# Graph transformer block on one core: node products every second closing gather, Q copies on ScalarE, penalty work on every second step

## The chip, the cores and the metric

The kernel is written by hand for one core of a Trainium2 chip. It uses five engines, each with its own queue of instructions executed in order: TensorE (PE in the profile, its weight loads PEld), VectorE (DVE), ScalarE (ACT), GpSimd (POOL) and SyncE (SP). The last two mostly issue DMAs here. Engines wait for each other on semaphores. The metric is the device time of one execution in microseconds (us).

## The reference

6250 nodes with 256 features, 200000 edges sorted by destination, 8 edge types. Two graph layers follow each other, both with a residual sum and a layer norm around them:

```python
xt = einsum('ni,rio->rno', x, weight)            # layer 0: 8 products for each node
out = segment_sum(xt[edge_type, src_col], row)   # summed over the edges of a node
x = _layernorm(x + relu(out + bias))

Q, K, V = x @ Wq, x @ Wk, x @ Wv                 # layer 1: attention over the edges, 8 heads
score = einsum('ehd,ehd->eh', K[src], Q[dst]) / sqrt(HD) + edge_bias
attn = softmax of score over the edges of each dst
x = _layernorm(x + block(attn-weighted sum of V[src], layer norms, FFN 256-1024-256))
```

## The kernel before, in words

The nodes are cut into W = 49 windows of 128. The program has one long first phase, then the edge phase of layer 1, then the dense part per node.

**Layer 0, gathers.** The edges are sorted by window into T = 1568 lists of 128; W = 49 more lists, the closing ones, hold what is left over of each window, so there are ITEMS = 1617. GpSimd issues an indirect DMA for each (L743, 128 rows of 256 floats) into a ring of 16 tiles in groups of four. TensorE multiplies each tile by a one-hot matrix (`total(i)`, L922) and VectorE adds the result to the window's row in `acc_w` (`add(i)`, L1125). `total` of a closing item waits until the add of the item two before it is done; there are two PSUM banks for them.

**The middle stage.** As soon as closing item j is added, window j is complete. For every window the stage does: on VectorE the relu and the residual sum (`relu_add`, L1329), batch statistics (`count` L1334, `moment` L1338), one over the deviation (`root` L1342) and the normalisation (`normal` L1346); on ScalarE the square root (`deviation`, L1581); on TensorE two transposes (`turn`, L1510), the K and V product (L1537, 512 columns) and the Q product (L1543, 256 columns), both in float32, which the profile shows as two passes for each product; on ScalarE the copy of the transposed tile (`turned`, L1570) and of K and V (L1595); on VectorE the copy of Q into `acc_w` (L1471). SyncE stores the normalised window (L1276, 128 KB) and K and V (L1278, 256 KB), and reloads a ring of x tiles (L1254).

The order of all this is written out by hand. VectorE's part is `norm(m)`: step m starts window m and finishes parts of the windows m-1 to m-7, `normal(m - 4)` and the Q copy of window m-7 among them. TensorE's part is `products(w)`, which begins with `turn(w + 1)`. Both are interleaved with the closing items by two rules that hang on `PACE`:

```python
LAG, PACE = 3, 3
def vector_step(i): return (j - LAG) // PACE if ... (j - LAG) % PACE == 0 else None
def tensor_step(i): return j // PACE - 7 if j is not None and j % PACE == 0 and j >= 7 * PACE else None
```

So `norm(m)` follows the add of closing item 3m (at item j = 3m + 3), and `products(w)` follows the total of closing item j = 3w + 21. The ten products 0 to 9 lie among the closing items, and the other 39 follow in a loop of their own; of the `norm` steps 16 lie among them and 40 behind.

ScalarE's loop over w has the order `deviation(w + 3)`, `turned(w + 1)`, the K and V copy of w, then from window 22 on three copies of turned edge records (`keep_records`, L1576). The K and V copy waits until the store of window w-2 has landed.

**Extra work in `norm` steps.** The edge phase needs tables that VectorE builds in between: constants (`select_consts`, step 16), the window of each item (`walk_row` L1390, steps 21 to 24, `walk_table` L1395 and L1397, step 25), the ends of the records (`pens_ends` L1401, step 26, which waits for 13 indirect DMAs of GpSimd, L1300), penalties (`pens_flag` L1409 and L1411, `pens_out` L1415 and L1417, steps 27 to 32 one after the other), `carries_out` (step 38), and five passes over the local offsets and weights (L1443, L1492, L1446, L1449, steps 44 to 50). On TensorE `spread` (L1515) follows the products of windows 13 to 16, and `turn_records` (L1527) those of windows 22 to 34.

When all five engines are through, a meeting (`meet`, L354) opens the edge phase. Its first gather is at L1664.

## Time and profile before

| | us |
|---|---|
| median of 3 runs | 6389.73 |
| fastest and slowest of them | 6384.63, 6389.86 |
| span of the profiled execution, first to last instruction | 5325.8 |
| TensorE busy / VectorE busy | 4332.7 (81%) / 4739.1 (89%) |
| ScalarE busy / GpSimd busy | 3258.1 (61%) / 3215.5 (60%) |
| granted TensorE clock, mean over the span | 0.965 |

The times are of runs without the profiler. The page gives no time of the profiled execution but its span. The runs' median lies 1063.9 us above the span, a factor of 1.1998.

### The profile page before, as it was taken

How to read it: one execution, taken by the hardware profiler on the slowest of the kernel's cores; microseconds unless marked ns; L12 is line 12 of the kernel's file. 1: busy time of each engine (PE TensorE's matmuls, PEld its weight loads, DVE VectorE, ACT ScalarE, POOL GpSimd, SP SyncE). 2: the span in 40 equal slices, each digit the busy share in tenths (PEclk: the TensorE clock that was granted, in tenths of full speed). 3: DMA queues.
4: the chain of work that ended last, by engine and by line, in shares of the span. 5: the costliest groups of instructions: out<-in, count | busy, mean ns of one | idle time of the engine just before them, and what ended most of it. 6: DMA issues, size and time to landing. Idle time of an engine off the chain costs nothing.

```text
span 5325.8 us, 88503 instructions
## 1 busy us (share of the span) xinstructions
PE 4332.7 (81%) x19115; PEld 2887.9 (54%) x19115; DVE 4739.1 (89%) x15510; ACT 3258.1 (61%) x8885; POOL 3215.5 (60%) x3370
## 2 busy tenths in 40 slices
PE   8997777777777777666978888888888888888997
PEld 3444444344444444443656666666666666666665
DVE  6888999999999999665679999999999999998666
ACT  3887777777777777300356666666666666663221
POOL 2003777777777777777167777777777777770000
PEclk9999999999999999877999999999999999999999
DMA  6333333333333333436567777777777777772000
GB/s 200 125 120 102 106 106 105 105 105 106 106 105 103 103 103 104 131 105 112 184 202 215 215 214 212 212 210 211 212 209 212 211 210 211 212 212 87 9 16 25
DMA packets 346045, 779.09 MB, mean 146 GB/s; under 512 B 75122, under 2 KB 176519, under 8 KB 345525
## 3 DMA queue, kind: packets, MB, share of 16 engines
q0 software_dynamic: 214608, 659.52, 43.4%
q1 hardware_dynamic: 127285, 111.00, 6.7%
q8 instruction: 174, 2.85, 0.2%
q10 hardware_dynamic: 3632, 2.88, 0.2%
q14 instruction: 346, 2.83, 0.2%
HBM read 691.52 MB, written 81.59 MB: 145 GB/s over the span
## 4 chain that ended last, share of the span: by engine, by line
PE 37%; DVE 29%; issue 16%; POOL 8%; ACT 4%; DMA 3%; DVEq 3%; SPq 0%; ACTq 0%; POOLq 0%
PE pb L1700 11%; POOL big L743 8%; DVE node_a L1848 5%; PE pb L922 4%; PE pb L1684 4%; PE pb L418 4%; DVE walk_s L1059 3%; ACT walk_s L752 3%; PE pb L2103 3%; PE pb L832 2%; DVE big L1804 2%; DMA big<-xt_table,big 2%; DVE big L1013 2%; DVE node_a L1125 2%; PE pb L2092 2%
## 5 line engine op out<-in xcount | busy, mean ns | idle before, releaser
L1664 POOL DMA_INDIRECT big<-kv_table,walk_s x1664 | 1585.2, 953 | 579.9 <-issue 477.8
L743 POOL DMA_INDIRECT big<-xt_table,big x1617 | 1554.6, 961 | 542.5 <-issue 457.0
L752 ACT ACTIVATE walk_s<-walk_s,big 128x128 bf16<-128x128 bf16 x4704 | 1498.8, 390 | 441.0 <-DVE walk_s L1059 416.4
L922 PE MATMUL pb<-big,walk_s 128*128 128x256 f32 x3234 | 1037.1, 416 | 225.0 <-DMA big<-xt_table,big 203.6
L1700 PE MATMUL pb<-big,early 128*128 128x264 f32 x3328 | 841.8, 397 | 98.9 <-issue 83.9
L1125 DVE TENSOR_TENSOR node_a<-node_a,pb 128x256 f32 (+1 forms) x1617 | 661.4, 410 | 209.0 <-PE pb L922 198.4
L1684 PE MATMUL pb<-node_a,hot_t 128*128 x3328 | 820.1, 390 | 29.9 <-issue 23.0
L832 PE MATMUL pb<-walk_s 128*128 128x384 bf16 x1568 | 534.1, 341 | 362.3 <-ACT walk_s L752 329.5
L922 PEld LDWEIGHTS pb<-big,walk_s 128*128 128x128 f32 x3234 | 616.1, 206 | 371.4 <-DMA big<-xt_table,big 277.4
L1700 PEld LDWEIGHTS pb<-big,early 128*128 128x128 f32 x3328 | 603.8, 192 | 220.5 <-issue 118.8
L1684 PEld LDWEIGHTS pb<-node_a,hot_t 128*128 128x128 f32 x3328 | 603.9, 191 | 113.4 <-issue 48.3
L832 PEld LDWEIGHTS pb<-walk_s 128*128 128x128 bf16 x1568 | 153.9, 98 | 824.1 <-ACT walk_s L752 773.0
L1757 ACT ACTIVATE early<-off_e,one_p 128x512 f32<-128x512 bf16 x416 | 300.3, 722 | 487.9 <-PE pb L1700 487.4
L1804 DVE TENSOR_TENSOR big<-big,pb 128x1024 f32<-128x1024 f32 x416 | 504.2, 1212 | 29.1 <-DMA big<-kv_table,walk_s 23.5
L1752 ACT ACTIVATE off_e<-iota_q,walk_s 128x128 bf16<-128x128 f32 x1664 | 525.8, 388 | 0.2
L834 PE MATMUL pb<-walk_s 128*97 128x384 bf16 x1568 | 523.3, 334 | 0.0
L1810 DVE TENSOR_REDUCE big<-big 128x32 f32<-128x1024 f32 x416 | 504.2, 1212 | 0.1
L1834 DVE TENSOR_TENSOR big<-big,pb 128x1024 f32<-128x1024 f32 x409 | 493.4, 1206 | 4.5 <-PE pb L1700 4.5
L1155 DVE TENSOR_SCALAR walk_s<-early,big 128x128 f32<-128x128 int16 x1570 | 472.6, 301 | 8.9 <-ACT node_a L791 7.5
L1059 DVE TENSOR_SCALAR walk_s<-early,big 128x225 bf16<-128x225 int16 x1568 | 473.0, 302 | 0.0
L1058 DVE TENSOR_SCALAR walk_s<-early,big 128x128 bf16<-128x128 int16 x1568 | 427.8, 273 | 39.2 <-PE pb L834 37.2
L1848 DVE SCALAR_TENSOR_TENSOR node_a<-node_a,walk_s,pb 128x264 f32 x832 | 397.6, 478 | 3.6 <-PE pb L1700 2.4
(294 smaller groups left out, 5573.2 us busy)
## 6 DMA issues: line engine op xcount, KB each, us to landing
xt_table<-big SPq DMA_DIRECT2D x98, 512.0 KB, 2.9
big<-kv_table,walk_s POOLq DMA_INDIRECT x1664, 3.7
big<-xt_table,big POOLq DMA_INDIRECT x1617
pens<-pen_table SPq DMA_DIRECT2D x832, 12.1 KB
kv_table<-big SPq DMA_DIRECT2D x49, 256.0 KB, 2.1
x_store<-big SPq DMA_DIRECT2D x49, 128.0 KB, 2.5
big<-in_x POOLq DMA_DIRECT2D x48, 128.0 KB, 3.3
big<-x_store SPq DMA_DIRECT2D x6, 1024.0 KB, 11.9
```

The source lines that it names most:

```text
L743: e.indirect_dma_start(sum_rows[:, q % SUM_ROWS, k, :], None, xt_table, bass.IndirectOffsetOnAxis(ap=idx_all[:, i:i + 1], axis=0))\
L752: ins = e.activation(hot_v[:, t % SORT_HOTS, v, :], hot_q[:, t % SORT_HOTS, :], ACT.Copy, scale=byte[:, t:t + 1])
L832: e.matmul(pb[:, 0, 0:3 * P], hot_c[:, t % SORT_HOTS, 0:P], vals, start=(u == 0), stop=last, skip_group_check=True)
L922: e.matmul(pb[:, bank, 0:D], one_hot, sum_rows[:, q % SUM_ROWS, k, :], start=True, stop=True)\
L1059: e.tensor_scalar(hot_c[:, k, 0:COLS], iota_s[:, 0:COLS], c_c[:, t:t + 1], None, ALU.is_equal)\
L1125: e.tensor_tensor(to, to, pb[:, bank, 0:D], ALU.add).then_inc(added.sem, 1)
L1664: e.indirect_dma_start(rows[:, q % ROW_RING, k, 0:2 * D], None, kv_table, bass.IndirectOffsetOnAxis(ap=src_i[:, i:i + 1], axis=0))\
L1684: ins = e.matmul(pb[:, q % 2 * 2 + k // 2, k % 2 * D:(k % 2 + 1) * D], hot_t[:, q % 2, k * P:(k + 1) * P], acc_q[:, bass.ds(at[k // 2], D) ...
L1700: ins = e.matmul(pb[:, 5 + j, 0:AW], hot_e[:, q % 2, i * P:(i + 1) * P], rows[:, q % ROW_RING, i, D:ROW], start=(k == 0), stop=(k == 1))
L1752: ins = e.activation(off_e[:, k * P:(k + 1) * P], iota_q[:, 0:P], ACT.Abs, bias=dl_f[:, i:i + 1], scale=-1.0)
L1804: e.tensor_tensor(keys, keys, pb[:, q % 2 * 2:q % 2 * 2 + 2, :].rearrange("p b (k n) -> p b k n", k=2), ALU.mult).then_inc(x_mul.sem, 1)
L1848: e.scalar_tensor_tensor(to, to, same_w[:, i:i + 1], pb[:, 5 + j, 0:AW], ALU.mult, ALU.add)\
```

## The change

`PACE` goes from 3 to 2. The Q copy leaves VectorE's `norm` for ScalarE's loop, directly behind the K and V copy. `SPREAD_AT` and `REC_AT` put the spreads and the turned records six windows later (19 and 28). VectorE's table work moves to later steps: `walk_row` 25 to 28, `walk_table` 30, `pens_ends` 31, the six penalty passes 32, 34, 36, 38, 40 and 42, `carries_out` 46. The last passes come behind the last normalisation, in steps 53 to 58.

```diff
-        LAG, PACE = 3, 3
+        LAG, PACE = 3, 2
...
-        NORM_LAG, Q_LAG = 4, 7
-        STEPS_MID = W + Q_LAG
-        REC_AT = 22
+        NORM_LAG = 4
+        SPREAD_AT, REC_AT = 19, 28
+        STEPS_MID = W + NORM_LAG + 6
...
-                w = m - Q_LAG
-                if 0 <= w < W:
-                    e.wait_ge(s_qkv, 2 * w + 2)
-                    e.tensor_copy(acc_w[:, w + 1, 0:D], pb[:, 4 + w % 2, 0:D]).then_inc(s_qc, 1)
...
-                if 21 <= m < 25:
-                    walk_row(m - 21)
-                if m == 25:
+                if 25 <= m < 29:
+                    walk_row(m - 25)
+                if m == 30:
                     walk_table()
-                if m == 26:
+                if m == 31:
                     pens_ends()
-                if 27 <= m < 33:
-                    k, odd = divmod(m - 27, 2)
+                if 32 <= m < 44 and m % 2 == 0:
+                    k, odd = divmod((m - 32) // 2, 2)
...
-                if m == 38:
+                if m == 46:
                     carries_out()
-                if m == 44:
+                late = m - W - NORM_LAG
+                if late == 0:
                     locals_of()
-                if m == 46:
+                if late == 1:
...
-                b = w - 13
+                b = w - SPREAD_AT
...
                 e.activation(kv_out[:, w % 2, :], pb[:, 2 + w % 2, :], ACT.Copy).then_inc(s_kvc, 1)
+                e.wait_ge(s_qkv, 2 * w + 2)
+                e.activation(acc_w[:, w + 1, 0:D], pb[:, 4 + w % 2, 0:D], ACT.Copy).then_inc(s_qc, 1)
```

What this moves, in the order of each engine's instructions. In the changed kernel the lines of the middle stage carry slightly other numbers (L1329 is L1330 there, L1543 is L1541, L1595 is L1593).

VectorE among the closing items, one step, before (L1329 to L1338 are the norm step, L1471 the Q copy, L1125 the adds of closing items):

```order
L1329 SCALAR_TENSOR_TENSOR big<-node_a,big 128x256
L1342 RECIPROCAL rstd<-spread_s 128x1
L1334 BN_STATS stats<-big 128x6
L1346 TENSOR_SCALAR big<-big,mv,rstd 128x256
L1338 BN_AGGR mv<-stats 128x2
L1471 COPY node_a<-pb 128x256
L1125 TENSOR_TENSOR node_a<-node_a,pb 128x256 x3
```

and now:

```order
L1330 SCALAR_TENSOR_TENSOR big<-node_a,big 128x256
L1343 RECIPROCAL rstd<-spread_s 128x1
L1335 BN_STATS stats<-big 128x6
L1347 TENSOR_SCALAR big<-big,mv,rstd 128x256
L1339 BN_AGGR mv<-stats 128x2
L1125 TENSOR_TENSOR node_a<-node_a,pb 128x256 x2
```

The copy has left the step, and two adds lie between norm steps instead of three.

ScalarE in the same place, two windows, before (L1595 is the K and V copy, L1581 the square root, L1570 the copy of the transposed tile):

```order
L1595 ACTIVATE big<-pb 128x512
L1581 ACTIVATE spread_s<-mv,eps_c 128x1
L1570 ACTIVATE big<-pb 128x256
L1595 ACTIVATE big<-pb 128x512
L1581 ACTIVATE spread_s<-mv,eps_c 128x1
L1570 ACTIVATE big<-pb 128x256
```

and now:

```order
L1593 ACTIVATE big<-pb 128x512
L1595 ACTIVATE node_a<-pb 128x256
L1579 ACTIVATE spread_s<-mv,eps_c 128x1
L1568 ACTIVATE big<-pb 128x256
L1593 ACTIVATE big<-pb 128x512
L1595 ACTIVATE node_a<-pb 128x256
L1579 ACTIVATE spread_s<-mv,eps_c 128x1
L1568 ACTIVATE big<-pb 128x256
```

The Q copy (L1595 there) stands between the K and V copy and the square root that the next norm step waits for.

VectorE at the first two penalty passes, before (L1409 and L1415 are the passes):

```order
L1409 TENSOR_TENSOR big<-big 128x13x127
L1329 SCALAR_TENSOR_TENSOR big<-node_a,big 128x256
L1342 RECIPROCAL rstd<-spread_s 128x1
L1334 BN_STATS stats<-big 128x6
L1346 TENSOR_SCALAR big<-big,mv,rstd 128x256
L1338 BN_AGGR mv<-stats 128x2
L1471 COPY node_a<-pb 128x256
L1415 TENSOR_SCALAR big<-big 128x13x127
```

and now:

```order
L1410 TENSOR_TENSOR big<-big 128x13x127
L1330 SCALAR_TENSOR_TENSOR big<-node_a,big 128x256
L1343 RECIPROCAL rstd<-spread_s 128x1
L1335 BN_STATS stats<-big 128x6
L1347 TENSOR_SCALAR big<-big,mv,rstd 128x256
L1339 BN_AGGR mv<-stats 128x2
L1330 SCALAR_TENSOR_TENSOR big<-node_a,big 128x256
L1343 RECIPROCAL rstd<-spread_s 128x1
L1335 BN_STATS stats<-big 128x6
L1347 TENSOR_SCALAR big<-big,mv,rstd 128x256
L1339 BN_AGGR mv<-stats 128x2
L1416 TENSOR_SCALAR big<-big 128x13x127
```

Two norm steps lie between two passes where one lay.

## Rows read from the trace of the kernel before

**Rows 1.** Windows of the middle stage: length, busy PE, PEld, DVE, ACT, POOL, PEclk, DMA, GB/s

```profile
2510.00:2556.00 46.00, 39.19 (x146) 24.78 (x145) 24.25 (x83) 10.46 (x27) 18.27 (x20) 1.00 0.52 159
2557.00:2575.00 18.00, 18.00 (x76) 11.73 (x75) 9.66 (x39) 5.81 (x15) 12.45 (x13) 1.00 0.84 275
...
2500.00:2680.00 180.00, 166.10 (x631) 104.05 (x629) 117.77 (x369) 63.86 (x185) 43.16 (x46) 1.00 0.57 177
```

**Rows 2.** Timeline of PE at closing items 12 to 14 and 21: start, duration

```profile
2501.41 1.91 PE L922 MATMUL pb<-big,walk_s 128*128 128x256 f32 x6 [1.15 <-DMA big<-xt_table,big]
...
2509.60 0.70 PE L922 MATMUL pb<-big,walk_s 128*128 128x256 f32 x2 [0.95 <-DVE node_a L1125]
...
2510.14 0.38 PE L1510 MATMUL pb<-ident,big 128*128 128x128 f32 x2
```

**Rows 3.** Timeline of PE, one whole step among the closing items

```profile
2551.04 0.38 PE L1510 MATMUL pb<-ident,big 128*128 128x128 f32 x2
2551.26 1.88 PE L1537 MATMUL pb<-big 128*128 128x512 f32 x4
2552.98 1.03 PE L1543 MATMUL pb<-big 128*128 128x256 f32 x4
2553.84 1.03 PE L922 MATMUL pb<-big,walk_s 128*128 128x256 f32 x4
2555.62 0.67 PE L922 MATMUL pb<-big,walk_s 128*128 128x256 f32 x2 [0.75 <-issue]
2556.13 0.38 PE L1510 MATMUL pb<-ident,big 128*128 128x128 f32 x2
```

**Rows 4.** Timeline of ACT and DVE in the same step

```profile
2553.18 0.60 ACT L1595 ACTIVATE big<-pb 128x512 f32<-128x512 f32 x1 [1.34 <-PE pb L1537]
2553.67 0.28 ACT L1581 ACTIVATE spread_s<-mv,eps_c 128x1 f32<-128x1 f32 x1
...
2553.99 0.16 DVE L1342 RECIPROCAL rstd<-spread_s 128x1 f32<-128x1 f32 x1 [1.99 <-ACT spread_s L1581]
...
2554.80 0.39 DVE L1471 COPY node_a<-pb 128x256 f32<-128x256 f32 x1
2555.11 0.74 DVE L1125 TENSOR_TENSOR node_a<-node_a,pb 128x256 f32<-128x256 f32 x2
```

**Rows 5.** Waits from 2557 to 2680: total us, times, longest

```profile
ACT big L1595 <- DMA kv_table<-big: 7.4, 3, 3.5
...
PEld pb L1510 <- DVE big L1346: 3.0, 4, 1.5
...
PEld pb L1515 <- DVE big L1390: 0.7, 1, 0.7
```

**Rows 6.** DVE groups of the same stretch: busy us, mean ns, idle before

```profile
L1411 DVE TENSOR_TENSOR big<-big 128x1664 f32<-128x1664 f32 x2 | 6.4, 3180 | 0.0
...
L1449 DVE TENSOR_TENSOR walk_s<-walk_s,big 128x1664 f32<-128x1664 f32 x2 | 3.8, 1880 | 0.0
...
L1446 DVE TENSOR_SCALAR big<-walk_s 128x1664 f32<-128x1664 f32 x2 | 2.0, 1017 | 0.0
```

**Rows 7.** Timeline of DVE, first and last instruction around the constants of step 16

```profile
2560.31 0.39 DVE L1473 MEMSET node_a<- 128x400 f32 x1
...
2562.60 0.43 DVE L1329 SCALAR_TENSOR_TENSOR big<-node_a,big 128x256 f32<-128x256 f32 x1
```

**Rows 8.** Timeline of ACT, copies of turned records

```profile
2601.79 0.61 ACT L1576 ACTIVATE walk_s<-pb 128x128 f32<-128x128 f32 x3
2602.26 0.32 ACT L1581 ACTIVATE spread_s<-mv,eps_c 128x1 f32<-128x1 f32 x1
```

**Rows 9.** L1300, the gathers of records: duration, first and last start; landing

```profile
L1300 POOL DMA_INDIRECT big<-edge_table,t_int x13: 944/946/1064, 2557.5 to 2572.7; - x13
...
DMA to landing us min/median/max: 3.3/5.7/7.0
```

**Rows 10.** Timeline, the last Q product and the first gather of the edge phase

```profile
2678.18 1.03 PE L1543 MATMUL pb<-big 128*128 128x256 f32 x4
...
2681.36 1.03 POOL L1664 DMA_INDIRECT big<-kv_table,walk_s  x1 [46.30 <-SPq L354]
```

More of the change, by code:

```diff
@@ L1234, in build @@
         assert x_marks[FIRST_LOADS] == X_RING and all((hi - 1) // X_RING == lo // X_RING for lo, hi in x_loads[:-1])
-        NORM_LAG, Q_LAG = 4, 7
-        STEPS_MID = W + Q_LAG
-        REC_AT = 22
+        NORM_LAG = 4
+        SPREAD_AT, REC_AT = 19, 28
+        STEPS_MID = W + NORM_LAG + 6
+        assert SPREAD_AT > (W - 1) // PACE - 7 and SPREAD_AT + 4 <= REC_AT and REC_AT + WALK_G < W
         def xs_of(w):
@@ L1486, in norm @@
                         pens_flag(k)
-                if m == 38:
+                if m == 46:
                     carries_out()
-                if m == 44:
+                late = m - W - NORM_LAG
+                if late == 0:
                     locals_of()
-                if m == 46:
+                if late == 1:
                     c(e.tensor_copy(dl_b, dl_f))
-                if m == 47:
+                if late == 2:
                     bias_mask(0.0, ALU.is_lt)
-                if m == 48:
+                if late == 3:
                     bias_add()
-                if m == 49:
+                if late == 4:
                     bias_mask(float(P), ALU.is_ge)
-                if m == 50:
+                if late == 5:
                     bias_add()
```

## The prediction

> **What bounds the kernel now.** I read the page first: no engine is full over the whole span, so the stage decides. The windows came next. All lines that the change touches work between 2500 and 2680 us, where PE is busy 166.1 of 180 us at full granted clock [rows 1]; VectorE, with 117.8 us, is not the bound. So the question is where PE's other 14 us are, and PE's timeline answers it. Among the closing items one step (turn, K and V, Q, three totals) takes 5.09 us from turn to turn [rows 3]; ten such places lie there. Its work is 2.80 us (2551.04 to 2553.84) for a window's products and 3 x 0.43 for the totals (four passes of L922 are 0.86 us apart from the next start, when nothing stalls), together 4.09. From the first turn of the ten (2510.14, [rows 2]) to the one behind them (2556.13) are 9 x 5.11 us. So 1.02 us of a mean step is not work; 0.08 of it is a handover that will stay (below), 0.94 is waiting.
>
> Why it is idle stands in ScalarE's and VectorE's rows [rows 4]. The K and V product ends at 2552.98; its copy starts 0.20 later, the square root 0.49 after that, and VectorE, which had waited 1.99 us for this root, starts at 2553.99. Root to moment takes 0.81, the Q copy 0.31, the first add 0.34, then PE gets its third total (2555.62) and, 0.51 later, the next turn. The whole ring is one step long: products of w release the norm step that stands ahead of the add that the total ahead of products w+1 waits for. Behind the closing items PE runs without a gap (2.80 us a window), except where VectorE is late with penalty passes: 3.0 us before turns and 0.7 before a spread by PEld's rows [rows 5]. From the last Q product (2678.18 + 0.86 = 2679.04) to the edge phase's first gather are 2.3 us [rows 10], which stay as they are: a store landing and the meeting.
>
> **The change, part by part.** The yardstick is the end of the last Q product, 2679.04.
>
> *Earlier start.* Products 0 now follow total 14 instead of total 21. Totals 12 to 14 ran from 2501.41 for 1.91 us, having waited for their rows to land; that wait stays. The turn can start at about 2503.3 instead of 2510.14 [rows 2]: 6.8 us earlier. Seven totals are then still to do, 7 x 0.43 = 3.0 us. Gain 3.8. VectorE can follow: a norm step without the copy is 0.81 + 0.34 (the relu sum has the size of an add), and two adds are 0.68, in all 1.83 us for two items [rows 4].
>
> *The ring opens.* With two items to a step, `norm(w + 6)`, which waits for the root behind products w-1, stands behind the add of item 2w + 12, and the total ahead of products w (item 2w + 14) needs that add alone. It does not wait for this norm step. So the ring is two steps long and holds one pass of about 5.4 us (worked out below), 2.7 for a step, against PE's 2.80 + 2 x 0.43 = 3.66. PE is the bound. The 0.94 us go in all nine steps between products 0 and 9: gain 8.5.
>
> *More handovers.* From the last total to the turn PE takes 0.51 us instead of 0.43 [rows 3]. There are 18 such places instead of 10: loss 8 x 0.08 = 0.6.
>
> *The Q copy on ScalarE.* 49 copies. ScalarE's copy of 512 columns takes 0.49 us to the next start, its copies of 128 take 0.47 / 3 = 0.16 each [rows 4, 8]; 256 columns lie between, 0.27. VectorE gives up 0.31 each, 15 us in all, but none of it at PE's bound outside the ring. The Trainium skill's page "Perfetto Trace Analysis", section Engine Utilization, gives ScalarE 153.6 and VectorE 245.76 G elements a second, a rule against this move: by it 32768 elements take 0.08 us longer on ScalarE, and each of the three late turns below would be later by that, 0.2 us in all. The rows show the fixed parts outweigh this. The square root behind the Q copy comes later: the copy waits for the Q product, 0.86 behind K and V, then 0.20 and 0.27, instead of 0.20 and 0.49. That is 0.64 us later. It is covered by the step gained above: PE needs the norm step a whole step later.
>
> *Penalties every second step.* Behind the closing items PE's step is 2.80, plus 0.33 while records are turned (three transposes at 0.11). VectorE's two steps with one long pass are 2 x 1.15 + 3.2 [rows 6] = 5.5 us, against PE's 5.6 to 6.3. Three such pairs are nearly even, so a few tenths may stay: I take 0.5 us. Of the 3.7 us that go, PE's own gaps between starts show about 3.4. Gain 2.9. The bounds are 0 (the waits stay, 3.4 lost) and 3.7.
>
> *Constants.* Step 16 now falls among the closing items (item 35). It holds VectorE for 2.3 us (2560.31 to 2562.60, [rows 7]), and the next two adds stand behind it. VectorE has 3.66 - 1.83 = 1.8 us to spare in a step, less what it waits for the root; I estimate 0.8 us lost, between 0.5 and 2.3.
>
> *Spreads and records six windows later.* The same instructions, cost 0. The gathers of records start behind the last add, now near 2567: 13 x 1.25 us, then 5.7 to land [rows 9], so at about 2589. `pens_ends` asks for them behind product 24, about 2593. If that margin of 4 us goes, VectorE stands and PE with it.
>
> *The last passes.* They come behind the last normalisation: three of 1.88 and three of 1.02 us [rows 6], 8.7 in all. The last normalisation can go 0.64 us later than before; PE then has the products of windows 47 and 48 ahead, the copy and the store. Before, that normalisation ended some 9.6 us ahead of 2679.04 and 11.9 ahead of the gather; now about 9.0 and 11.3. 8.7 us fit with 2 us to spare. Cost 0; without cover each us beyond it shows in full.
>
> Sum: 3.8 + 8.5 - 0.6 + 2.9 - 0.8 = 13.8, so **14 us** off the span of 5325.8. Direct count as a check: 2503.3 + 49 x 2.80 + 34 x 0.43 + 18 x 0.08 + 3 spreads of 0.89 and one of 0.22 + 13 x 0.33 + 1.3 of waits - 0.22 (the last has no turn) = 2664.9, or 14.1 less than 2679.04.
>
> **From the span to the time.** The median is 1063.9 us above the span, a factor of 1.1998. If what lies around the span is fixed, the time falls by 14; if all stretches by that factor, by 16.8. The trace cannot tell. I take the factor, since the trace shows no stretch outside the program's own work that could be a fifth of it, and keep 14 as the other end. The Trainium skill, "Advanced Engine Details and Errata", section Clock Domains, says that a chip's power profile moves the base clock and names 2.0 beside 2.4 GHz for PE, a factor of 1.2; no row here shows that the timed chip was set so. Forecast: 6389.7 - 16.8 = **6373**.
>
> **The rivals.**
>
> *DMA holds the shorter step.* A step would move 2 x 128 KB of rows, 128 of x1, 256 of K and V and about 128 of x, some 0.79 MB in 3.66 us: 215 GB/s instead of 159. For it: ScalarE waited 7.4 us for K and V stores in the stretch with 275 GB/s at 0.84 of the DMA engines [rows 1, 5]. Against it: by the same row 215 GB/s are 0.66 of them, and PE lost nothing to those waits. If a step took 4.3 us, 17 steps would cost 10.9 us more; gain 3 x 1.2 = 3.7, time 6386. The store would have to land later than about 6 us after its issue.
>
> *Records late.* If the record gathers land in 13 us instead of 5.7, `pens_ends` holds VectorE about 3 us: gain 11 x 1.2 = 13, time 6377. For it: they now share the DMA engines with stores at PE's full rate; against it, they did before too.
>
> *The ring stays closed (slower).* If the norm step ahead of each product still needs the product just before, the Q copy on ScalarE is in the ring. It is then 1.72 (K and V) + 0.86 + 0.20 + 0.27 + 0.29 (to the root) + 0.81 + 0.34 + 0.17 + 0.51 + 0.22, about 5.4 us for two items instead of three. Products 17 would start at 2503.3 + 17 x 5.4 = 2595.1, and 31 more at 2.80 with 7.5 of spreads and records and 1 of waits end near 2693: 14 us later, time 6389.7 + 16.8 = 6406. It decides as soon as a step's slack (3.66 x 2 against 5.4, so 1.9 us) is eaten, say by a late add. The order rows speak against it.
>
> **How the numbers follow.** A measurement of this kernel can tell a difference of about 0.2%, 12.8 us. The forecast gets 0.74: of that 0.70 lie beyond 12.8 us, 0.04 fall short with the factor absent and two terms at their low ends. DMA holds: 0.14, all within 0.2%. Records late: 0.06, 0.02 faster and 0.04 within. Ring closed: 0.06, slower. Faster 0.72, same 0.22, slower 0.06. The range: the best case is all terms at their high ends (start at 2502.9, no waits left, constants 0.5), 15.7 x 1.2 = 18.9 us, and 2.5 of scatter between runs: 6368. At the other end it takes in records late and the milder half of the DMA case, 6382. That leaves out about 0.15.
>
> **What would show it.** Right: from one L1541 row to the next among closing items 3.7 us, no DVE-released idle before L922; the first L1508 turn of window 1 near 2503; the last Q product near 2665; VectorE's last pass ends before the first gather; ScalarE's Q copies start 0.2 behind L1541. Wrong: steps of 4 us or more with ScalarE waiting for stores, or the gaps before L1508 at the penalty passes as long as before; and if all of this holds but the time falls by 14 and not 17, the factor is wrong.

## The result, and the profile after

| | median us | range of the runs |
|---|---|---|
| before, 10 runs | 6389.8 | 6373.9 to 6414.2 |
| after, 10 runs | 6359.6 | 6344.3 to 6383.4 |

The ratio is 0.9952, 95% interval 0.9939 to 0.9965: faster by 30 us (22 to 39). Forecast were 6373 and a range from 6368. The direction is right; the gain is nearly twice the forecast's 17 us, and the time is 8.4 us under the range.

One thing must be known to read the numbers: the runs came in sets of different pace, in which the kernel before takes about 5328, 6390 or 6474 us, run after run. Below, a quick, 6390 or 6474 chip is short for such a set. Whether the pace belongs to the chip isn't shown, since the record gives the 6390 and the 6474 set of the experiments the same chip number. The profile shown ahead of the prediction (span 5325.8) is of the quick kind, the times beside it are of the 6390 kind. In each of the ten runs after, the time is 1.7 to 1.8 us above the span of the same run, so the 1063.9 us between the two were never around the program.

The profile after is of the 6390 kind. Its page begins:

```profile
span 6363.5 us, 88501 instructions
...
PEclk9998888888888888768888888988899888899999
```

Its granted TensorE clock is 0.82 in the gather stage and 0.89 in the edge phase; in the profile before it was 0.93 and 0.99. Its windows (gather stage, touched stage, edge phase, dense last part):

```profile
480.00:2935.00 2455.00, 1636.90 (x6063) 973.02 (x6063) 1834.34 (x8320) 1308.96 (x4067) 1526.58 (x1587) 0.82 0.31 87
2935.00:3115.00 180.00, 167.96 (x629) 107.30 (x629) 98.10 (x309) 77.97 (x231) 46.15 (x49) 0.95 0.55 177
3118.00:5836.00 2718.00, 2043.97 (x9222) 1550.09 (x9223) 2083.26 (x3675) 1428.19 (x3378) 1579.05 (x1664) 0.89 0.57 165
5836.00:6360.00 524.00, 465.21 (x1791) 321.00 (x1790) 365.61 (x1244) 129.90 (x275) 0.76 (x1) 0.97 0.11 32
```

VectorE's busy time in the touched stage fell from 117.8 us [rows 1] to 98.1, ScalarE's rose from 63.9 to 78.0: 49 copies changed sides. PE's timeline, a whole step among the closing items (answers [rows 3]) and the step with the constants:

```profile
2952.47 1.03 PE L1541 MATMUL pb<-big 128*128 128x256 f32 x4
2953.34 1.03 PE L922 MATMUL pb<-big,walk_s 128*128 128x256 f32 x4
...
2956.14 1.03 PE L1541 MATMUL pb<-big 128*128 128x256 f32 x4
...
2985.45 1.03 PE L1541 MATMUL pb<-big 128*128 128x256 f32 x4
2986.94 1.13 PE L922 MATMUL pb<-big,walk_s 128*128 128x256 f32 x4 [0.47 <-DVE node_a L1125]
...
2989.85 1.03 PE L1541 MATMUL pb<-big 128*128 128x256 f32 x4
```

A step is 3.67 us from Q product to Q product, with no idle time; the one with the constants is 4.40. ScalarE and VectorE in the same kind of step (answers [rows 4]):

```profile
2957.20 0.38 ACT L1595 ACTIVATE node_a<-pb 128x256 f32<-128x256 f32 x1 [0.27 <-PE pb L1541]
2957.48 0.28 ACT L1579 ACTIVATE spread_s<-mv,eps_c 128x1 f32<-128x1 f32 x1
...
2957.80 0.16 DVE L1343 RECIPROCAL rstd<-spread_s 128x1 f32<-128x1 f32 x1 [1.80 <-ACT spread_s L1579]
...
2958.60 0.72 DVE L1125 TENSOR_TENSOR node_a<-node_a,pb 128x256 f32<-128x256 f32 x2
```

VectorE still waits 1.8 us for the root, but PE no longer waits for VectorE. The end of the stage (answers [rows 10]): the last pass ends at 3114.61, 2.85 us ahead of the gather, and hides.

```profile
3112.72 1.89 DVE L1450 TENSOR_TENSOR walk_s<-walk_s,big 128x1664 f32<-128x1664 f32 x1
...
3114.30 1.03 PE L1541 MATMUL pb<-big 128*128 128x256 f32 x4
...
3117.46 1.03 POOL L1664 DMA_INDIRECT big<-kv_table,walk_s  x1 [22.84 <-SPq L354]
```

So the mechanism came as forecast. The question is the size: where the other 13 us are from.

### The profile page after: what moved, and what is told of

The parts are those of the page before. It is cut to its first block, busy times and chain, and to the rows that moved or that the text cites. A ratio compares the mean times of both kernels' runs of the same rounds, so it can differ in the third digit from the quotient of the medians.

```text
span 6363.5 us, 88501 instructions
## 1 busy us (share of the span) xinstructions
PE 4755.2 (75%) x19115; PEld 3163.2 (50%) x19115; DVE 4764.5 (75%) x15461; ACT 3290.1 (52%) x8934; POOL 3213.0 (50%) x3370
## 3 DMA queue, kind: packets, MB, share of 16 engines
q8 instruction: 174, 2.85, 0.2%
## 4 chain that ended last, share of the span: by engine, by line
PE 27%; issue 13%; DVE 8%; another core or an unknown queue 5%; DVEq 2%; ACT 2%; DMA 0%; POOL 0%; ACTq 0%; SPq 0%; POOLq 0%
PE pb L1700 11%; PE pb L1684 6%; PE pb L2103 2%; DVE node_a L1848 2%; PE pb L2092 2%; PE pb L922 1%; PE pb L1535 1%; DVEq L336 1%; ACT early L1743 1%; PE pb L2115 1%; PE pb L1675 1%; DVE big L1804 1%; PE pb L1726 1%; PE pb L1541 1%
## 5 line engine op out<-in xcount | busy, mean ns | idle before, releaser
L1664 POOL DMA_INDIRECT big<-kv_table,walk_s x1664 | 1580.4, 950 | 1161.8 <-PE pb L1700 537.6
L743 POOL DMA_INDIRECT big<-xt_table,big x1617 | 1556.5, 963 | 996.7 <-issue 454.1
L922 PE MATMUL pb<-big,walk_s 128*128 128x256 f32 x3234 | 1168.4, 457 | 156.5 <-DVE walk_s L1155 74.3
L1700 PE MATMUL pb<-big,early 128*128 128x264 f32 x3328 | 993.4, 449 | 205.1 <-issue 156.7
L1125 DVE TENSOR_TENSOR node_a<-node_a,pb 128x256 f32 (+1 forms) x1617 | 668.0, 414 | 588.4 <-PE pb L922 245.6
L832 PE MATMUL pb<-walk_s 128*128 128x384 bf16 x1568 | 590.3, 377 | 687.6 <-ACT walk_s L752 478.4
L1684 PE MATMUL pb<-node_a,hot_t 128*128 x3328 | 879.9, 410 | 23.4 <-issue 18.9
L1700 PEld LDWEIGHTS pb<-big,early 128*128 128x128 f32 x3328 | 688.1, 219 | 386.8 <-issue 261.3
L922 PEld LDWEIGHTS pb<-big,walk_s 128*128 128x128 f32 x3234 | 700.3, 232 | 320.5 <-issue 106.6
L1684 PEld LDWEIGHTS pb<-node_a,hot_t 128*128 128x128 f32 x3328 | 651.1, 207 | 124.8 <-issue 43.6
L834 PE MATMUL pb<-walk_s 128*97 128x384 bf16 x1568 | 583.0, 372 | 0.0
```

Of the source, the lines that this page charges most:

```text
L743: e.indirect_dma_start(sum_rows[:, q % SUM_ROWS, k, :], None, xt_table, bass.IndirectOffsetOnAxis(ap=idx_all[:, i:i + 1], axis=0))\
L832: e.matmul(pb[:, 0, 0:3 * P], hot_c[:, t % SORT_HOTS, 0:P], vals, start=(u == 0), stop=last, skip_group_check=True)
L834: ins = e.matmul(pb[0:COLS - P, 1, 0:3 * P], hot_c[:, t % SORT_HOTS, P:COLS], vals, start=(u == 0), stop=last, skip_group_check=True)
L922: e.matmul(pb[:, bank, 0:D], one_hot, sum_rows[:, q % SUM_ROWS, k, :], start=True, stop=True)\
L1125: e.tensor_tensor(to, to, pb[:, bank, 0:D], ALU.add).then_inc(added.sem, 1)
L1664: e.indirect_dma_start(rows[:, q % ROW_RING, k, 0:2 * D], None, kv_table, bass.IndirectOffsetOnAxis(ap=src_i[:, i:i + 1], axis=0))\
```

## The experiments

The comparison below uses one stretch, from the start of the 20th last row gather (L743) to the first edge gather (L1664). All that the change touches lies in it or just before its start. In the profile before it is 172.0 us; the forecast is 14 less.

**Four kernels on a quick chip** (kernel before: 5328.0 us, 33 runs). Run 1 is the kernel before, unchanged.

> The kernel before, unchanged, to get its trace in the condition in which the changed kernel was traced (span 6363.5 us, where the first trace of the kernel before had 5325.8). Theory A (pauses): its span is near 6385, its engines show pauses of 2 to 5 us that no other engine's work explains, and its middle stage, from the first closing total to the first gather of the edge phase, is 25 to 35 us longer than the changed kernel's (about 190 us): the closed ring of one step passes every pause on to TensorE, the open one takes part of it up. Theory B (elsewhere): the middle stages differ by 14 us as forecast and the rest of the 30 us lies in the two long stages around it. Time: no change, 6389 us.

Measured 5327.8 us, ratio 1.0001 (0.9992 to 1.0010), span 5321.7. The kernel repeats within 0.1%. It fell into a quick set, so it couldn't show how the kernel before looks where it takes 6390 us, and neither theory was decided.

Run 2 is the changed kernel with the Q copies back on VectorE, at their old lag:

```
                if 0 <= m - 2 < W:
                    moment(m - 2)
+                w = m - 7
+                if 0 <= w < W:
+                    e.wait_ge(s_qkv, 2 * w + 2)
+                    e.tensor_copy(acc_w[:, w + 1, 0:D], pb[:, 4 + w % 2, 0:D]).then_inc(s_qc, 1)
...
-                e.wait_ge(s_qkv, 2 * w + 2)
-                e.activation(acc_w[:, w + 1, 0:D], pb[:, 4 + w % 2, 0:D], ACT.Copy).then_inc(s_qc, 1)
```

> The changed kernel with the Q copy back in the norm step of VectorE (seven steps behind, as before). Both theories: the closing steps stay at 3.67 us, since VectorE has room for 0.31 us more in a step. The late passes now share VectorE with the last Q copies and cannot end before the last Q product and copy, so VectorE ends some 5 us behind TensorE and the stage's end moves by about 4 us. If the copy's place matters only there: 4 x 1.2 = 5 us slower than the changed kernel, 6365 us. If moving the copy had been worth its 15 us of VectorE time: 6375 us.

Measured 5318.5 us, ratio 0.9984 (0.9975 to 0.9993), stretch 163.8 us. PE's steps among the closing items are 3.66 us as with the copy on ScalarE, so the pace opens the ring by itself. But the late passes now end after PE. Timelines of its end:

```profile
2666.01 1.03 PE L1545 MATMUL pb<-big 128*128 128x256 f32 x4
...
2667.14 0.42 DVE L1472 COPY node_a<-pb 128x256 f32<-128x256 f32 x1 [1.22 <-PE pb L1545]
...
2671.52 1.89 DVE L1450 TENSOR_TENSOR walk_s<-walk_s,big 128x1664 f32<-128x1664 f32 x1
...
2673.74 1.03 POOL L1666 DMA_INDIRECT big<-kv_table,walk_s  x1 [27.61 <-DVEq L354]
```

The last Q copy waits for the last Q product, the passes queue behind it, and the edge phase meets them at 2673.4. From last Q product to gather are 7.7 us instead of 3.2. So the move to ScalarE is worth 4.5 us at this place. The stretch is 6.2 us longer than that of the changed kernel in run 10 (157.6): another 1.6 us are longer waits at the penalty passes, where VectorE has 0.31 us more to do for each window. Without the move over a third of the 16.2 us that the whole change gains on a quick chip is given back.

Run 3 has the new places (spreads, records, penalty steps, late passes) with the old pace and the Q copies on VectorE. Against the changed kernel, with the lines of the Q copy as in run 2:

```
-        LAG, PACE = 3, 2
+        LAG, PACE = 3, 3
...
+                w = m - 7
...
```

> The kernel before with the table work of VectorE, the spreads and the turned records at their new places alone (PACE 3, Q copy on VectorE). The closed ring stays: steps among closing items 5.1 us. The waits at the penalty passes go (2.9 us), but the late passes end some 5 us behind the last Q product and give it back. Theory A: no change within 5 us, 6389 us. A theory in which the spread penalty work is the source of the surplus gain: 6370 us or less.

Measured 5330.3 us, ratio 1.0002 (0.9993 to 1.0011), stretch 180.2. The steps are 5.07 as before, and the same 4.5 us stand at the end. The new places alone gain nothing.

Run 4 is the changed kernel with the old pace:

```
-        LAG, PACE = 3, 2
+        LAG, PACE = 3, 3
```

> The changed kernel with PACE 3 again (Q copy on ScalarE, table work at its new places). The closed ring is back and holds the wait for the Q product: steps of 5.4 us instead of 5.1, nine of them, 3 us; the waits at the penalty passes are gone, 3 us. So as before or up to 3 us slower: 6389 to 6393 us under theory A, where nearly all of the 30 us is the pace. If the pace is worth only what the forecast gave it (11 of 14 us), the time is 6376.

Measured 5329.8 us, ratio 1.0004 (0.9995 to 1.0013), stretch 177.2. In the closed ring the Q copy on ScalarE costs. One step in its timelines:

```profile
2521.53 1.03 PE L1541 MATMUL pb<-big 128*128 128x256 f32 x4
2522.39 1.03 PE L922 MATMUL pb<-big,walk_s 128*128 128x256 f32 x4
2524.52 0.70 PE L922 MATMUL pb<-big,walk_s 128*128 128x256 f32 x2 [1.10 <-DVE node_a L1125]
...
2526.99 1.03 PE L1541 MATMUL pb<-big 128*128 128x256 f32 x4
...
2522.59 0.38 ACT L1595 ACTIVATE node_a<-pb 128x256 f32<-128x256 f32 x1 [0.27 <-PE pb L1541]
2522.88 0.29 ACT L1579 ACTIVATE spread_s<-mv,eps_c 128x1 f32<-128x1 f32 x1
```

The step takes 5.46 us here, 5.40 in the mean, against 5.07: the root is later by 0.64, the copy's 0.31 on VectorE is saved, 0.33 remain. Pace two is what gains; pace three with the rest of the change gains nothing.

**Four kernels on a 6390 chip** (kernel before: 6390.0 us, 27 runs). Run 5 is the changed kernel again:

> The changed kernel once more, unchanged. On a chip that runs the kernel before in about 5328 us (as the first four runs did) the middle stage's terms alone decide. Theory A (the change is worth the 14 us of the middle stage, and the surplus came with the slow-paced execution): 5314 us, ratio 0.9973, last Q product 160 us behind the first (before 166). Theory B (the change is worth 30 us anywhere): 5298 us, ratio 0.9944. If the chip runs the kernel before in about 6390 us again: A and B both 0.995, and the trace must say in which stage the surplus lies.

Measured 6366.0 us, ratio 0.9966 (0.9949 to 0.9983): 24 us, and 11 to 33 by the interval. Stretch 165.1, as in the first profile after (165.2). Its first step among the closing items is a long one, though the ring is open:

```profile
2945.75 1.03 PE L1541 MATMUL pb<-big 128*128 128x256 f32 x4
...
2949.66 1.19 PE L922 MATMUL pb<-big,walk_s 128*128 128x256 f32 x2 [2.15 <-issue]
...
2955.96 1.12 PE L1541 MATMUL pb<-big 128*128 128x256 f32 x4
```

It is 10.21 us instead of 3.66.

Run 6 is the kernel before with nothing changed but the Q copies, which go to ScalarE (the lines of run 2 the other way round, pace three):

> The kernel before with the Q copies on ScalarE alone (three items to a step, penalty passes as before). The ring is closed, so the copy's place in it counts: ScalarE's square root comes 0.64 us later, VectorE's copy of 0.31 is gone, so a step of the ten is 5.07 + 0.33 = 5.40 us, 9 x 0.33 = 3.0 us more; behind the closing items VectorE gains 0.31 a window, which takes about 1 us off the penalty waits. Expected +2 us (0 to +3), 5330 us, ratio 1.0004. The rival, that the Q copy is a burden of VectorE which PE pays for: a step of 4.8 us, 3 us less, 5325.

Measured 6389.4 us, ratio 0.9993 (0.9978 to 1.0008). Behind a first step of 11.35 us the steps are 5.38 to 5.47, as expected (5.40), and the rival's 4.8 is out. Its stretch takes 190.0 us: 24.8 more than the changed kernel's on that chip, where I had 14, or 16 with this kernel's own loss of about 2 us.

Runs 7 and 8 have stalls of VectorE put in, first the kernel before, then the changed one:

```
+                if m in (7, 9, 11, 13):
+                    for _ in range(4):
+                        c(e.memset(acc_w[:, :, D:AW], 0.0))
```

> The kernel before with four artificial stalls of 1.86 us on VectorE (four 0.46 us memsets of the same columns behind norm steps 7, 9, 11 and 13, while products 1 to 7 run). If the ring is closed, each is paid in full: 4 x 1.86 = 7.4 us, 5335.4 us, ratio 1.0014, and four of the ten steps become 6.9 us instead of 5.1. If VectorE has room in a step (it waits 2 us for the root), nothing: 5328 us.

Measured 6397.6 us, ratio 1.0014 (1.0000 to 1.0029): 7.5 us more, at the edge of what these runs can tell.

> The changed kernel with the same four stalls of 1.86 us behind norm steps 7, 9, 11 and 13, again while products 1 to 7 run. If the ring is two steps long and holds 5.4 us of 7.3, a stall is absorbed: at most 0.3 us each, so at most 1.2 us above the changed kernel (5315 us against 5314). If the ring is closed at heart and only shorter, each is paid in full: 7.4 us, 5321 us. The difference between what the stalls cost before and after (7.4 against 1) is what an open ring saves where an engine pauses.

Measured 6362.8 us, 3 us under run 5 and not told apart from it (ratio to before 0.9957, 0.9941 to 0.9974). The answer is in the traces. The memsets stand 0.54 apart, so a stall is 2.17 us and not 1.86. In the kernel before (run 7) the last stalled step is 7.24 us instead of 5.07: paid in full. The other three are longer, 8.88, 8.72 and 9.80 us. PE's timeline of the third and the fourth, and the windows behind their waits:

```profile
3001.74 1.19 PE L922 MATMUL pb<-big,walk_s 128*128 128x256 f32 x2 [3.08 <-issue]
...
3003.16 3.62 PE L1540 MATMUL pb<-big 128*128 128x512 f32 x4
...
3016.45 0.70 PE L922 MATMUL pb<-big,walk_s 128*128 128x256 f32 x2 [2.88 <-DVE node_a L1125]
...
3017.20 1.88 PE L1540 MATMUL pb<-big 128*128 128x512 f32 x4
```

```profile
3001.70:3006.60 4.90, 4.86 (x9) 2.54 (x10) 1.03 (x3) 0.38 (x1) 0.00 (x0) 0.50 0.05 13
3016.40:3020.00 3.60, 3.55 (x13) 2.37 (x14) 1.15 (x4) 1.16 (x3) 0.00 (x0) 1.00 0.00 0
```

PE waited 2.9 to 3.1 us in all four. Behind three of these waits the granted clock was 0.50 to 0.61, the K and V product took 2.68 to 3.62 us instead of 1.88, and VectorE got its root later; behind the fourth it stayed at 1.00. The four stalls, 8.7 us in all, cost PE 14.4 us.

In the changed kernel (run 8) the first stall falls into the long first steps and can't be read. The other three make steps of 4.35 us instead of 3.67: 0.69 each, more than the 0.3 expected, a third of the stall. VectorE's total of two steps, 2 x 1.83 + 2.17, is 5.8 of 7.3 us, but the stalled step alone (4.0) is longer than PE's. PE's waits there are 0.42 us, and the granted clock stays at 1.00.

**Four kernels on a quick chip again** (kernel before: 5329.8 us, 21 runs). Run 9 is the kernel before, run 10 the changed one.

> The kernel before, unchanged, for its stages beside the next run's. If this chip paces the gather stages slowly (6390 us): from the start of the 20th last row gather (L743) to the first edge gather (L1664) 185 to 190 us, where a quick chip takes 172 to 174; ratio 1.000. On a quick chip 5328 us and 172 to 174.

Measured 5327.5 us, ratio 0.9995 (0.9986 to 1.0004), stretch 175.1.

> The changed kernel, unchanged. Theory A (the terms of the middle stage are right, and the surplus of the first result is what a slow-paced chip adds to a slower start and a closed ring, plus scatter between executions of the untouched stages): on a slow-paced chip 20 to 24 us less than the run of before from the 20th last row gather to the first edge gather, and differences of either sign and under 10 us in the two stages on its sides; ratio about 0.9963. On a quick chip 14 us less in that stretch and in the whole, ratio 0.9973. Theory B (something in the gather or edge stages gets faster with the change): the stretch gives 14 us on either chip, and 10 us or more come again from one and the same untouched stage.

Measured 5308.3 us (5 runs), ratio 0.9964 (0.9950 to 0.9977): 19 us, 12 to 27. The stretch of run 9 and then of this one, in the windows' columns:

```profile
2508.70:2683.80 175.10, 161.56 (x618) 101.79 (x617) 111.88 (x349) 63.38 (x183) 36.11 (x39) 1.00 0.56 175
```

```profile
2505.00:2662.60 157.60, 154.38 (x605) 100.29 (x603) 92.99 (x290) 76.56 (x225) 36.68 (x40) 1.00 0.60 192
```

PE stands still for 3.2 of 157.6 us, where it was 13.5 of 175.1. The three quick traces of the kernel before (172.0, 174.2, 175.1) have a mean of 173.8, so the change takes 16.2 off it. Everything outside the stretch (span less stretch) took 5155.3 us in run 9 and 5148.6 in this one. The other seven quick traces lie between 5147.5 and 5155.2, those of the kernel before among them. So no change of the stages around it is seen.

Run 11 is the kernel before with products w behind item 3w + 18 instead of 3w + 21:

```
-            return j // PACE - 7 if j is not None and j % PACE == 0 and j >= 7 * PACE else None
+            return j // PACE - 6 if j is not None and j % PACE == 0 and j >= 6 * PACE else None
...
-                if i == T + 6 * PACE:
+                if i == T + 5 * PACE:
...
-            for w in range((W - 1) // PACE - 6, W):
+            for w in range((W - 1) // PACE - 5, W):
```

> The kernel before with one thing changed: products w follow item 3w + 18 instead of 3w + 21 (still every third item). The total ahead of products w then needs only adds ahead of norm step w + 5, whose root stands behind products w - 2, so the ring is two steps long at this pace too. If the ring was what held the step: steps of 2.80 + 3 x 0.43 + 0.08 = 4.17 us instead of 5.07, ten times, 9 us, and 1.6 us of an earlier start: 11 us, 5317 us on a quick chip, ratio 0.998. If the pace of three was at fault (VectorE's three adds and a norm step), steps of 5.07 stay and 1.6 us are gained: 5326 us, ratio 0.9997.

Measured 5321.5 us, ratio 0.9990 (0.9981 to 0.9999), stretch 165.6: 8.2 us less than 173.8, where 11 were expected. The steps are 4.45 us, neither 5.07 nor 4.17. PE's and VectorE's timelines tell why:

```profile
2533.51 1.81 PE L922 MATMUL pb<-big,walk_s 128*128 128x256 f32 x6
2535.16 0.38 PE L1510 MATMUL pb<-ident,big 128*128 128x128 f32 x2
...
2534.15 0.85 DVE L1125 TENSOR_TENSOR node_a<-node_a,pb 128x256 f32<-128x256 f32 x2 [1.37 <-PE pb L922]
```

Three totals take 1.65 us, 0.55 each, not 0.43. There are two banks, so the third waits for the add of the first, 0.28 us more than forecast for the step. Of the old step of 5.07 the ring cost 0.62 and the third total 0.28. The 0.94 that the prediction gives to the ring, from a mean step of 5.11, had these two parts, and a pace of two removes both.

Run 12 is the changed kernel with the same shift, to item 2w + 12, and the constants moved behind the closing items (steps 23 and 24):

> The changed kernel with products w behind item 2w + 12 instead of 2w + 14, and the constants of step 16 behind the closing items (the memset in step 23, the others in step 24). Two items' worth of earlier start, of which PE waited some 1 to 2 us for rows, and the 0.74 us of the constants: 2 us better than the changed kernel on a quick chip (5312 us, ratio 0.997), 3 us on a slow-paced one. The step of 4.40 us at product 10 becomes 3.66. If the norm step ahead of the turn is late instead, steps of 4 us or more between products, and no gain.

Measured 5313.1 us (5 runs), ratio 0.9965 (0.9951 to 0.9978); stretch 156.2 against 157.6. All seventeen closing steps are 3.66 or 3.67. But the turn behind the last one waits, since its norm step stands behind the last add of the phase and not behind the add of item 46:

```profile
2567.46 0.44 PE L1509 MATMUL pb<-ident,big 128*128 128x128 f32 x2 [1.59 <-DVE big L1347]
```

The 2 us that were expected on top of the changed kernel don't show: run 10 took 5308.3 us in the same set.

**Four kernels on a 6474 chip** (kernel before: 6474.2 us, 27 runs). Run 13 is the kernel before again, run 14 the changed one.

> The kernel before, unchanged. On a quick chip: 5328 us, the stretch from the 20th last row gather to the first edge gather 172 to 175.1 us as in three traces so far. On a slow-paced chip: 6390 us and 185 to 190 us in that stretch.

Measured 6471.0 us, ratio 1.0002 (0.9990 to 1.0015), stretch 186.2.

> The changed kernel, unchanged. If the surplus is scatter of the untouched stages: the stretch takes 157 to 159 us on a quick chip (16 less than before), 165 on a slow-paced one (20 to 24 less), and the stages on its sides differ by under 8 us with a sign that changes between pairs. If the change reaches them: 5 us or more less in the same stage as in the pairs so far (the last dense part was 3 us shorter in the tenth run, the gather stage 6 us shorter on the slow-paced chip).

Measured 6442.2 us, ratio 0.9959 (0.9944 to 0.9974), stretch 167.1. The windows of run 13 and then of this one, gather stage, stretch, edge phase:

```profile
479.00:2992.00 2513.00, 1640.84 (x6079) 978.31 (x6080) 1839.09 (x8336) 1307.95 (x4070) 1532.36 (x1598) 0.82 0.31 86
2992.00:3177.00 185.00, 165.20 (x617) 103.62 (x615) 112.49 (x349) 63.17 (x183) 35.73 (x39) 0.98 0.52 165
3178.00:5940.00 2762.00, 2055.49 (x9225) 1558.29 (x9222) 2082.55 (x3675) 1428.00 (x3378) 1575.13 (x1664) 0.88 0.57 162
```

```profile
479.00:3001.00 2522.00, 1644.27 (x6094) 984.67 (x6095) 1840.93 (x8342) 1310.40 (x4076) 1529.02 (x1598) 0.82 0.31 85
3001.00:3167.00 166.00, 157.79 (x602) 101.73 (x600) 92.92 (x290) 75.98 (x225) 36.25 (x39) 0.98 0.57 182
3167.00:5916.00 2749.00, 2052.14 (x9221) 1555.53 (x9222) 2081.20 (x3675) 1425.23 (x3377) 1575.07 (x1663) 0.88 0.57 163
```

The stretch is 19 us shorter; the stages beside it differ by +9 and -13. Both are more than the 8 expected, but of opposite sign, and neither stage differs the same way in all pairs of traces. Run 16 below is the same kernel as this one, and its gather stage and edge phase differ from this one's by 11 and 16 us: so large is the scatter of stages that nobody touched.

Run 15 is the kernel of run 12 with the late norm step put right and the constants in steps 25 and 26:

```
+            m = (W - 1 - LAG) // PACE + 1
             for i in range(ITEMS - LAG, ITEMS):
                 add(i)
-            for m in range((W - 1 - LAG) // PACE + 1, STEPS_MID):
+                if closing(i) == PACE * m:
+                    step.norm(m)
+                    m += 1
+            for m in range(m, STEPS_MID):
                 step.norm(m)
...
```

> The twelfth kernel (products w behind item 2w + 12) with norm step 23 behind the add of item 46, where the pattern has it, instead of behind the last add, and the constants in steps 25 and 26, where a step of PE is 3.69 us. The turn that waited 1.59 us behind norm step 23 in the twelfth run waits for nothing: the stretch 154.7 us instead of 156.3 on a quick chip (the changed kernel: 157.6), 3 us less than the changed kernel in all, 5310 us, ratio 0.9967. If something else holds that turn, 156.3 stays.

Measured 6450.5 us, ratio 0.9974 (0.9961 to 0.9987). The turn waits no more: the step that was 5.47 us in run 12 is 3.66. The stretch is 164.9, 2.2 and 2.8 us under those of runs 14 and 16, but the time isn't lower. A gain of 3 us is below what these runs can tell, so it doesn't count as a better version. Run 16 is the changed kernel once more.

> The changed kernel once more, so that two traces and two sets of times of it stand beside each other: as the fourteenth, within 0.1% of it in time; the stretch within 2 us of the fourteenth's.

Measured 6448.7 us, ratio 0.9967 (0.9956 to 0.9978), stretch 167.8; within 0.1% of run 14, as expected.

## Why the prediction was right in kind and wrong in size

| chip (kernel before) | stretch before | stretch after | less | all outside it, before / after | time, less |
|---|---|---|---|---|---|
| 5328 | 172.0, 174.2, 175.1 | 157.6 | 16.2 | 5147.5 to 5155.3 / 5148.6 | 19 (12 to 27) |
| 6474 | 186.2 | 167.1, 167.8 | 18.8 | 6280.2 / 6275.8, 6279.9 | 27 (17 to 36), 21 (14 to 29) |
| 6390 | 190.0 (Q copies on ScalarE) | 165.2, 165.1 | 24.8 | 6198.4 / 6198.3, 6196.1 | 31 (22 to 39), 22 (11 to 33) |

The last column is worked out from the ratios. Their mean, weighted by the intervals, is 0.38%: 20 us of 5328, 24 of 6390.

On a quick chip the terms can be checked one by one. They add up to 16.2 us where 13.8 were forecast.

*Earlier start, 3.8.* Right, and a little more. The first K and V product starts 0.9 to 2.7 us behind the 20th last gather before and 5.8 ahead of it after: 7.7 earlier in the mean, forecast 6.8.

*The ring opens, 8.5, and handovers, -0.6.* Right in cause, and a little more in size. PE's step is 3.66, forecast 3.74: there is no handover cost at two totals. What I called a handover of 0.08 is not seen there. This gives most of another 1.2 us. Run 11 shows the other misreading: 0.28 of the old wait was the third total in a row, not the ring. Both go, so the sum is hardly touched.

*Q copy on ScalarE, 0.* Right for the closing steps: run 2 has 3.66 us there with the copy on either engine, because the ring is open. Where it is closed, the copy on ScalarE costs 0.33 a step (runs 4 and 6), 3 us in all. What the prediction doesn't say is that the late passes hide only because the copy has left VectorE (run 2: 4.5 us at the end). The Trainium skill's page "Perfetto Trace Analysis", section Engine Utilization, gives peak rates by which, as an estimate, the copy would be 0.08 us longer on ScalarE. The rows don't show it: 0.28 to 0.29 to the next start there, 0.31 on VectorE [rows 4].

*Penalties, 2.9.* Nearly right: 3.2. In run 10 two turns wait 0.23 and 0.60, and with the weight loads behind these waits PE's steps there are 1.3 us longer than their work, where a rest of 0.5 was forecast. Against this the wait at the spread, which goes as well, was longer than the profile before had it. PE waited 0.32, 1.12 and 1.86 us in the three quick traces; this is the one of run 9:

```profile
2580.47 1.16 PE L1515 MATMUL pb<-ident,big 128*128 128x128 f32 x8 [1.86 <-DVE big L1390]
```

*Constants, -0.8.* 0.74 (4.40 against 3.66). *Late passes, 0.* Right: forecast 2 us to spare, measured 2.9.

None of the rivals came. With a step of 3.66 us DMA didn't hold it (4.3) and the ring wasn't closed (5.4), and `pens_ends` waited for its records in no trace of the changed kernel. Three sums of the prediction are slightly off, and nothing hangs on them: the closed ring's 2693 needs 32 products and not 31, the direct count gives 2664.8, and the terms named for the best case add up to 15.0 or 15.3 and not 15.7.

*From the span to the time.* **This is the step that failed.** I multiplied 14 by 1.1998, as if every stretch were longer by a fifth, with 14 as the other end. Neither holds. The gather stage (first to 20th last gather) goes from 2027 to between 2470 and 2522 us, the edge phase from 2119 to between 2705 and 2764, the dense last part takes 524 to 529 everywhere, and the touched stretch of the kernel before goes from 174 to 186. So the surplus has its places, and it doesn't scale the terms: outside the pauses PE's steps of 5.07, 3.66 and 2.80 us are the same on every chip. The other value, the fixed 1063.9 us around the span, falls too, by the 1.8 us at most that lie between a run's time and its own span. The Trainium skill, "Advanced Engine Details and Errata", section Clock Domains, from which a PE clock of 2.0 instead of 2.4 GHz could have been taken, isn't what is seen: four K and V products take 1.88 us at full granted clock on all three chips.

What takes the factor's place are pauses in which several engines stand at once (last section), and a slower start. From the first to the last K and V product the kernel before takes 166.7 us on a quick chip and 177.7 on the 6474 one, 11.0 more; the changed kernel 158.2, and 167.4 and 168.1, so 9.2 and 9.9 more. The pauses take about the same from both kernels, and 1 to 2 us less from the changed one. The start makes more of a difference on one of the slow chips. It comes 7.7 us earlier with the change on a quick chip, 8.8 on the 6474 chip, and 10.4 and 13.6 on the 6390 chip. The kernel before has seven more totals to do ahead of its first product, and totals seem to be slower there: two of them fewer (runs 12 and 15) bring the start forward by 3.2 us on a quick chip and by 4.4 on the 6474 one. No run tests this alone.

That an open ring takes up such pauses, as it does with the stalls put in, isn't shown. On the 6474 chip the first step of the kernel before took 10.43 us instead of 5.07 and the changed kernel's 3.67, but in run 5, on the 6390 chip, the changed kernel's took 10.21 instead of 3.66, and in run 6 of the same set, whose ring is closed, 11.35 instead of 5.39. The open ring lost 6.55 us there and the closed one 5.96.

The 24.8 us of the 6390 chip are too much by the loss of run 6, some 2 us, since no undisturbed trace of the kernel before exists from there; the time of run 6 is equal (0.9993).

The rest of the miss is the range. I allowed 2.5 us for scatter, from three runs. Ten runs of one kernel on that chip spread over 39 us, and two medians of the changed kernel there lie 6 us apart (6359.6, 6366.0). Even the mean gain, 24 us, would have ended over 2 us under the range. Between the 22 to 25 us in the stretch and 30 in the first result nothing is shown but scatter, and the interval of that result reaches down to 22.

## What to carry to other kernels

Ask how many steps long a ring is, not only how long its pass is: the same norm step cost PE 0.6 us in each of nine steps while it stood ahead of the add that the next products wait for, and nothing two steps away. A closed ring also passed a stall of VectorE on in full (2.17 of 2.17), and in three of four cases with a lower granted clock on top, where the open one passed on a third (0.69). And before scaling a gain by time over span, find out in which stages the difference lies; where the profile can't say, let the range hold every reading of it, and the scatter of more than three runs.

## What was not expected of the hardware

The same program takes 5328, 6390 or 6474 us from set to set. VectorE's and ScalarE's instructions are equally long in all (the adds of L1125 in the mean 0.410 us on the quick chip and 0.414 on the 6474 one). PE's matmuls are longer on a slow chip, as its granted clock in the gather stage is 0.82 there instead of 0.93: those of L922 take 0.457 us in the mean instead of 0.416. What grows most is the time in which the engines wait. Part of it goes in pauses of several engines at once. The timelines of run 14, at the spreads:

```profile
3066.73 1.05 PE L1513 MATMUL pb<-ident,big 128*128 128x128 f32 x8
3067.62 0.38 PE L1508 MATMUL pb<-ident,big 128*128 128x128 f32 x2
...
3077.17 0.69 PE L1508 MATMUL pb<-ident,big 128*128 128x128 f32 x2 [5.70 <-issue]
...
3077.92 3.78 PE L1535 MATMUL pb<-big 128*128 128x512 f32 x4
...
3075.39 0.69 DVE L1391 TENSOR_TENSOR big<-big,pb 128x512 f32<-128x512 f32 x1 [9.77 <-remote]
...
3077.48 0.38 ACT L1568 ACTIVATE big<-pb 128x256 f32<-128x256 f32 x1 [9.34 <-issue]
...
3072.20 0.95 POOL L1301 DMA_INDIRECT big<-edge_table,t_int  x1 [0.30 <-issue]
3073.46 0.95 POOL L1301 DMA_INDIRECT big<-edge_table,t_int  x1 [0.30 <-issue]
```

PE had finished the spread that VectorE was to subtract (L1513) and the turn that ScalarE was to copy (L1508) by 3068.0, and the two started 7.6 and 9.5 us later; GpSimd, which waits for nobody in that stretch, kept its 1.25 us. So engines that hand work to each other stood, and the one that doesn't ran on. All nine traces of the slow-paced kinds have such a pause at the gathers of records. But pauses aren't all of it. Those of over 1.5 us in which PE, VectorE and ScalarE all stand add up to 34 us in the gather stage and edge phase of run 9 and to 210 in those of run 13, whose span is 1136 us longer.

In these rows the lower clock follows the pause and doesn't make it. From 3060 to 3070 the granted clock is 1.00, and from 3077 to 3083, behind PE's 5.70 us of waiting, it is 0.50, the 1.2 GHz level: the K and V product takes 3.78 us, twice its 1.88. Run 7 shows the same behind waits that only the stalls made. So a wait of PE can cost more than its own length. What makes the pauses stays open: no run here changed them.
